# Value products of two key tiles in one burst at every fourth slot, in a decoder layer with a state-space mixer and grouped attention

## The reference

```python
x = x + mixer(layernorm(x))           # projections, a causal conv of 4 taps, silu, a scan over time,
                                      # y * silu(z), projection back
x = x + attention(layernorm(x), ctx)  # 32 query heads, 8 key heads, depth 16; keys = values = ctx
x = x + experts(layernorm(x))         # 16 experts, 2 per token, and a shared one

scores  = einsum('bkgsd,bktd->bkgst', qh, kh) / 4
weights = softmax(scores, axis=-1)
out     = einsum('bkgst,bktd->bkgsd', weights, vh)    # the value products
```

## Time and profile before

| | |
|---|---|
| median of 3 runs | 1396.94 us (1394.41 to 1400.47) |
| the profiled execution | 1399.34 us, its span 1397.5 us |
| TensorE busy | 1253.2 us (90%) |
| VectorE busy | 694.0 us (50%) |
| ScalarE busy | 465.2 us (33%) |
| mean granted TensorE clock | 0.952 |

### The profile page before, as it was taken

The page is one execution under the profiler, slowest core; times in us unless marked ns, Lnnn a source line. Parts: engine busy times, 40 slices in busy tenths (PEclk is TensorE's granted clock), DMA queues, the critical chain, the costliest instruction groups (busy, mean ns, idle before and its releaser), DMA issues. The chain is left out here.

```text
span 1397.5 us, 14980 instructions
## 1 busy us (share of the span) xinstructions
PE 1253.2 (90%) x5077; PEld 515.8 (37%) x5078; DVE 694.0 (50%) x1049; ACT 465.2 (33%) x661; POOL 242.0 (17%) x420
## 2 busy tenths in 40 slices
PE   5989899998999999899999989999778999999930
PEld 2434433333434333343333333333333444444410
DVE  4634495566475546467555757665373111111125
ACT  1310334333554333455333544555211222222210
POOL 3010212110310201211210221111001111111135
PEclk9998999899999979899999999999989999999975
DMA  6322682003534102263200442000062335664247
GB/s 174 92 77 61 158 155 63 27 12 91 124 90 88 38 12 72 50 130 84 63 12 12 110 80 44 23 2 31 22 240 67 131 126 180 225 234 172 83 137 253
DMA packets 101232, 134.40 MB, mean 96 GB/s; under 512 B 13362, under 2 KB 72882, under 8 KB 98866
## 3 DMA queue, kind: packets, MB, share of 16 engines
q1 hardware_dynamic: 85778, 96.37, 26.1%
q0 software_dynamic: 6320, 20.71, 5.2%
q10 hardware_dynamic: 9072, 16.52, 3.1%
HBM read 104.34 MB, written 28.84 MB: 95 GB/s over the span
## 5 line engine op out<-in xcount | busy, mean ns | idle before, releaser
L606 DVE TENSOR_REDUCE mx<-ps_m 128x2 f32<-128x1024 f32 x256 | 313.3, 1224 | 283.7 <-PE ps_m L1029 279.9
L752 ACT ACTIVATE prob<-ps_s 128x1024 f32<-128x1024 f32 x256 | 262.2, 1024 | 433.2 <-PE ps_s L1012 433.1
L956 PE MATMUL acc<-xnT,wring 128*128 128x512 f32 x560 | 280.4, 599 | 2.4 <-DVE xz L538 1.8
L1630 PE MATMUL ps_gu<-ring,xgT 128*128 x376 | 179.2, 600 | 8.7 <-issue 6.7
L1012 PE MATMUL ps_s<-q_stack,k_stack 99*128 99x512 bf16 x512 | 157.9, 390 | 7.5 <-DMA q_stack<-mT 4.5
L1029 PE MATMUL ps_m<-k_stack,q_stack 96*128 96x512 bf16 x512 | 157.6, 389 | 5.6 <-DVE mx L606 5.2
L1445 DVE COPY xgT<-ps_x 128x512 f32<-128x512 f32 x47 | 32.5, 692 | 230.4 <-PE ps_x L1604 230.4
L1042 PE MATMUL ps_o<-prob,values 128*32 128x512 f32 x1024 | 140.7, 622 | 0.0
L956 PEld LDWEIGHTS acc<-xnT,wring 128*128 128x128 f32 x560 | 102.6, 190 | 67.3 <-issue 33.2
L1012 PEld LDWEIGHTS ps_s<-q_stack,k_stack 99*128 99x128 bf16 x512 | 36.0, 97 | 193.9 <-issue 143.0
L1630 PEld LDWEIGHTS ps_gu<-ring,xgT 128*128 128x128 f32 x376 | 67.7, 192 | 79.6 <-issue 79.6
(11 more groups left out here) (234 smaller groups left out, 1213.6 us busy)
## 6 DMA issues: line engine op xcount, KB each, us to landing
ring<-in_w_experts SPq DMA_DIRECT2D x16, 1536.0 KB, 8.7
wring<-in_w_in SPq DMA_DIRECT2D x80, 256.0 KB, 3.4
q_stack<-part_rows SPq DMA_DIRECT2D x96, 128.0 KB, 4.6
list_y<-y ACTq DMA_DIRECT2D x47, 256.0 KB, 2.0
wring<-in_w_out SPq DMA_DIRECT2D x32, 256.0 KB, 2.8
part_rows<-part SPq DMA_DIRECT2D x20, 384.0 KB, 3.2
xt<-in_x SPq DMA_DIRECT2D x16, 256.0 KB, 3.7
out<-res ACTq DMA_DIRECT2D x16, 256.0 KB, 4.0
```

Of the source, the lines that this page charges most:

```text
L606: nc.vector.tensor_reduce(mx[:, n % G, 2 * u:2 * u + 2], ps_m[:, :, :], AX.X, ALU.max).then_inc(s_max, 1)
L752: nc.scalar.activation(prob[:, slot % PROB, :, :], ps_s[:, :, :], ACT.Exp, scale=SCALE).then_inc(s_exp, 1)
L956: ins = nc.tensor.matmul(bank(b, n), weights, xnT[:, k, :], start=(k == 0), stop=(k == KD - 1))
L1630: ins = nc.tensor.matmul(ps_gu[p][:, :], xgT[:, p, k * P:(k + 1) * P], weights(own)[:, k * 2 * F:(k + 1) * 2 * F], start=(k == 0), stop=(k ...
```

## The change

In slots 4 to 164 the products are issued at every fourth slot, those of two key tiles at once; from slot 167 on they stand where they stood.

```diff
-                if slot >= 3 and slot % 2 == 1 and (slot - 3) // 2 < 2 * R * G * TB // 2:
+                if 4 <= slot <= FRONT and slot % 4 == 0:
+                    products(slot // 2 - 2)
+                    products(slot // 2 - 1)
+                if slot > FRONT + 1 and slot % 2 == 1 and (slot - 3) // 2 < 2 * R * G * TB // 2:
                     products((slot - 3) // 2)
```

## The result

| | before | after |
|---|---|---|
| median | 1394.25 us (12 runs, 1389.82 to 1407.35) | 1406.74 us (12 runs, 1401.88 to 1412.38) |
| ratio | | 1.0077, 95% interval 1.0048 to 1.0106 |
| profiled execution, span | 1399.34, 1397.5 us | 1403.57, 1401.8 us |
| mean granted clock of that execution | 0.952 | 0.958 |

The change makes the kernel 0.77% slower, 10.7 us (by the ratio on record; the two medians lie 12.5 us apart). The forecast was 7.2 us.

A forecast was written before the change was run, and what follows sets the result against it. TensorE's own sequence was taken to set the time. Terms -9.4 + 11.2 + 4.4 + 1.0 = +7.2 us, added to the runs' median of 1396.94, gave 1404 us; range 1398 to 1412.

The forecast's parts named there:

- The gain: TensorE, slots 4 to 164: each of 41 joins saves 0.23 us of entering and leaving the strip form, 9.4 us.
- z waits for silu: z projection, m = 32 to 40: without the set TensorE waits for silu_z; 3.7 us a batch, 11.2 in all.
- Heads to inner: Slots 144 to 148 and like stages: two sets leave the shadow of VectorE's chain; 4.4 us lost, bounds 2.2 to 6.6.
- The token transposes: Slots 101 and 102, batches 2 and 3: step projection waits for the last copy; 0.5 us each, 1.0 lost.
- ScalarE is no danger: Ring of six probability slots: places are freed two slots before the exponential wanting them, and needed exponentials already waited for.
- no new wait comes from these: ScalarE's exponentials and the emptying of ps_o: the change was to add no wait there.
- What costs nothing: Convolution and output projection, m = 5 to 31 and 49 to 63: VectorE has slack, only the gain is felt.
- More or less half clock: Two rivals on TensorE's clock: a fifth half-clock stretch, +12 us, 1409, chance 0.12; a stretch gone, 1394, chance 0.14.
- the prediction's own sign of being wrong: Wrong if z waits are missing, a joined burst takes over 2.1 us, or half-clock stretches differ by more than one.
- The bounds: Whole sum, with each loss at its ends and the gain kept: +4 to +14 us.

The follow-up runs named there:

- e1: The change without its joins at m = 32, 36 and 40 (32 joins instead of 41); 1395.15 us, ratio 0.9969 to the kernel before.
- e2: The change with silu_z ahead of the reduction of the same slot on VectorE; 1393.08 us, ratio 0.9946 to the kernel before.
- e7: The kernel before with bursts joined at m = 32, 36 and 40 only, 9 joins; 1401.02 us, ratio 1.0009.
- e10: The kernel before with four unread float32 matmuls in TensorE's wait at m = 44 of batches 1 to 3; 1383.07 us, ratio 0.9901.
- e12: The change with four unread float32 matmuls in TensorE's wait at m = 44; 1404.65 us, ratio 1.0051 to the kernel before.

## Why the prediction was right, and in what it was off

The direction and the mechanism were right, and the time, 1406.74, lies in the range. That it lies within 3 us of 1404 is in part luck: the sum fell 3.5 us short, while the kernel before, whose three runs gave 1396.94, has a median of 1394.25 over twelve. By its steps:

- **The gain, 41 x 0.23 = 9.4.** Measured 0.24 for a join in ordinary slots, 9.8 us. The joined burst costs 1.95, as worked out from the head means.
- **z waits for silu, 11.2.** Measured 3.74 a batch, 11.2; the single wait 0.77 against 0.78, and the second pass 0.10 late. e1, e2 and e7 show it from three sides: leaving these joins out, removing the wait they lay bare, and making them alone.
- **Heads to inner, 4.4.** Under-sized. The three stages together grew by 5.35 with six joins worth 1.4 in them, so 6.8 us, just over the upper bound of the step (6.6). I took half the price in two batches because half clock would cover it. Before and after have the same time at half clock in this stage, and at full clock each of the three would be 1.5 to 2.0 us longer with its two joins, 2.0 to 2.5 without, by the estimate above: about the full price of two sets, in every batch.
- **The token transposes, 1.0.** About 0.6, and not by the wait that was named. Before and after have different half clock here, but two other runs have none in slots 36 to 44 (m = 0 to 7 of batch 2): e10, with the sets where they were, and e1, with the joins. The scores of slots 36 and 44, first in e10, then in e1:

```profile
321.66 0.60 PE L1017 MATMUL ps_s<-q_stack,k_stack 99*128 99x512 bf16 x2
...
351.09 0.61 PE L1017 MATMUL ps_s<-q_stack,k_stack 99*128 99x512 bf16 x2
```

```profile
323.26 0.59 PE L1012 MATMUL ps_s<-q_stack,k_stack 99*128 99x512 bf16 x2
...
352.50 0.60 PE L1012 MATMUL ps_s<-q_stack,k_stack 99*128 99x512 bf16 x2 [1.07 <-ACT prob L752]
```

They are 29.43 and 29.24 us, and slots 100 to 108 of the change, at full clock too, 29.25. Two joins should have saved 0.48 and saved 0.19: 0.3 a batch is lost, 0.6 in all. The step projection waits for the last copy in one batch only (0.35). The loss is the net of more: the new wait of 1.07 for ScalarE at m = 8, against a wait of 1.19 before the transposes of slot 41 that is gone. "ScalarE is no danger", with "no new wait comes from these", is a step of the prediction that failed; it cost little here because the other wait went with it.

- **"What costs nothing."** Not quite: in two groups of four slots around m = 16 the change has +0.11 and +0.20 where others have -0.24, 0.8 us together. In the one looked at, the scores wait for a transfer of the row maxima (0.20 printed): the set that stood between slots 55 and 56 had covered its landing. In the profile of e12 both groups have their full -0.24, so this term comes and goes with the execution.
- **More or less half clock.** By the number of stretches the prediction's own sign of being wrong was met: it allowed one more or less, and from 208 to 785 us the change has six where there were four. But they are shorter, 34 us together against 48, hence only 4.2 us between the two executions. Over its runs the change has a mean clock of 0.954; its companions have none on record, and the other groups of the kernel before have 0.953 to 0.955. So neither rival is seen in the change as it stands. But e12 against e10 shows that this is no law: with the wait at m = 44 filled, the kernel before keeps full clock at the heads and the change does not, and it costs 21.6 us.
- **The bounds.** By the terms as written the lower one is -9.4 + 10.3 + 2.2 + 0 = +3.1, not +4; nothing hangs on it.

With the terms as measured, -9.8 + 11.2 + 6.8 + 0.6 + 0.8 = +9.6 us, beside 10.7 measured (6.7 to 14.8 by its interval). Of the 3.5 us by which the forecast was short, the heads' term makes 2.4.

## What to carry to other kernels

Work that stands between two dependent steps of another engine's chain is a cover, and its price in the profile is not its worth: before moving it, compare the moment at which its successor's data are ready with the moment at which the successor would start without it. Here 0.24 us were saved at each of 41 joins, and 0.87 lost at each of nine waits that were laid bare and 1.09 at three more in the z projection alone. A cover can also stand before an engine that was not looked at, as ScalarE at m = 8. Joining only where the slack is longer than what moves, and letting VectorE release the waiting engine before it starts a long reduction, turns the sign. And when differences of half a percent are read, separate the clock from the work first.

## What the runs showed of the hardware that was not expected

- A wait of 1.91 us of TensorE, in a stage of short and narrow matmuls, was followed by half clock in two of three batches (0.71 in the window of batch 2; it begins 3.1 and 4.0 us after the scores of m = 44), and four useless matmuls in that wait took it away in all three and made the kernel 1% faster. The Trainium skill (TensorE: Matmul & The Clock Gate, "A second HAM failure mode: psum-queue depth-cycling") says that frequent short idles between groups of matmuls can make the clock swing. The heads' stage of e12, where half clock follows a wait of 1.08 us in all three batches (0.83 to 0.87 in the windows), agrees with it in so far as a short idle is enough; the z stage of the change, with its 0.77 us of waiting in every second slot, does not: no half clock begins between slots 68 and 80 there.
- A wait costs TensorE more than its row prints: 0.62 us printed were 0.77 of delay, and 0.10 more in the second pass of the float32 matmul behind it.
- Half clock for 1 us cost 0.46 us in the heads' stage of before (4.66 us for 10.2, 9.33 for 20.5), a little less than half.
- Entering and leaving the form of four column strips costs 0.24 us together, and a whole-array float32 matmul between two such bursts is 0.10 longer.
